# A macaron transformer layer on 8 cores: Q projections fed between the attention windows, double-buffered LayerNorm operands

## What is computed

```python
x = x + 0.5 * ffn(layernorm(x), W_base, b_base, W_router, A, B)
x = x + attn(layernorm(x), Wq, Wk, Wv, Wo)
x = x + 0.5 * ffn(layernorm(x), W_base, b_base, W_router, A, B)

# attn: one K and V head of 128, 32 Q heads of 128, rope on Q and K
for i in range(0, S, 256):                    # windows of 512 tokens
    scores = Qw @ Kw.T * SCALE
    attn = sigmoid(scores); attn = attn / attn.sum(-1)
    wout = attn @ Vw
    # the first half is blended linearly with the last window's second half
return out @ Wo.T
# ffn: x @ W_base.T + b_base + top-2-of-8 gated rank-16 experts
```

## Time and profile before

| | us |
|---|---|
| median of 2 timed runs | 6466.22 (6465.81 to 6466.63) |
| profiled execution, its own time | 6366.92 |
| its span on the slowest core, core 3 | 6365.4 |
| spans of the eight cores | 6328.9 to 6365.4 |

### The profile page before, as it was taken

One profiled execution on the slowest core, in us unless ns is written; L12 is line 12 of the kernel. 1 busy time (PEld: TensorE's weight loads), 2 busy tenths in 40 slices (PEclk: granted clock), 3 DMA queues, 4 the chain that ended last, 5 costly groups with the idle time before them and its releaser, 6 DMA issues.

```text
span 6365.4 us, 39250 instructions; the slowest of 8 cores (6328.9 to 6365.4 us)
## 1 busy us (share of the span) xinstructions
PE 3416.1 (54%) x14036; PEld 1491.5 (23%) x14036; DVE 1207.2 (19%) x1986; ACT 1159.6 (18%) x1401; POOL 523.8 (8%) x900
## 2 busy tenths in 40 slices
PE   2379998344444444444444444444444444425999
PEld 1234443222222111222111222211122211112444
DVE  3511111531121001121100112100121210033111
ACT  3311111322111001212100121100121110022222
POOL 0001111100000110000111000011100011110111
PEclk7689999666665555666665666565666665656999
DMA  4335554321101332100233110133211023332776
GB/s 107 91 96 172 174 168 146 99 75 35 32 27 51 107 107 81 37 27 27 91 107 108 41 37 27 50 104 106 84 30 37 27 83 107 106 110 75 206 200 194
DMA packets 641074, 570.84 MB, mean 90 GB/s; under 512 B 35953, under 2 KB 568690, under 8 KB 640626
## 3 DMA queue, kind: packets, MB, share of 16 engines
q1 hardware_dynamic: 556914, 283.07, 16.5%
q0 software_dynamic: 83968, 285.27, 14.3%
HBM read 459.18 MB, written 109.05 MB: 89 GB/s over the span
## 4 chain that ended last, share of the span: by engine, by line
DMA 35%; PE 32%; DVE 13%; issue 8%; ACT 8%; DVEq 2%; POOL 1%; SPq 0%; POOLq 0%; ACTq 0%
DMA arena<-x2h 13%; PE PS L408 11%; DMA x2h<-arena 10%; PE PS L543 8%; DMA arena<-wqT 5%; DMA arena<-x1h 4%; PE PS L588 4%; PE PS L573 4%; DVE arena L659 3%; DMA out<-arena 2%; ACT arena L577 2%; PE PSM L202 2%; DVEq L47 2%; ACT arena L580 2%; ACT arena L249 2%
## 5 line engine op out<-in xcount | busy, mean ns | idle before, releaser
L652 PE MATMUL PS<-arena 128*128 128x512 bf16 x2048 | 885.9, 611 | 973.1 <-DVE arena L659 966.5
L408 PE MATMUL PS<-arena 128*128 128x512 bf16 x5120 | 1138.1, 381 | 38.6 <-ACT arena L249 25.7
L249 ACT ACTIVATE arena<-arena 128x512 bf16<-128x512 f32 (+1 forms) x784 | 581.2, 765 | 2847.4 <-PE PS L652 1635.0
L543 PE MATMUL PS<-arena 128*128 128x512 bf16 x2048 | 510.5, 416 | 443.6 <-ACT arena L249 407.3
L408 PEld LDWEIGHTS PS<-arena 128*128 128x128 bf16 x5120 | 501.6, 98 | 650.9 <-issue 53.8
L652 PEld LDWEIGHTS PS<-arena 128*128 128x128 bf16 x2048 | 261.3, 136 | 1595.2 <-issue 1587.7
L659 DVE TENSOR_TENSOR arena<-PS,arena 128x512 f32<-128x512 f32 x256 | 177.1, 692 | 1732.6 <-DMA arena<-x2h 1289.5
L202 PE MATMUL PSM<-arena 128*1 128x256 bf16 x1024 | 188.8, 370 | 426.1 <-ACT arena L197 333.8
L43 POOL DMA_DIRECT2D x2h<-arena x256 | 139.6, 545 | 3358.3 <-DVE arena L659 3353.7
L588 PE MATMUL PS<-arena 128*128 128x130 bf16 x2048 | 246.4, 311 | 299.6 <-ACT arena L580 299.6
L543 PEld LDWEIGHTS PS<-arena 128*128 128x128 bf16 x2048 | 212.8, 105 | 735.7 <-issue 538.0
(11 more groups left out here) (85 smaller groups left out, 1879.2 us busy)
## 6 DMA issues: line engine op xcount, KB each, us to landing
arena<-wbaseT SPq DMA_DIRECT2D x256, 512.0 KB, 6.4
arena<-wqT SPq DMA_DIRECT2D x256, 256.0 KB, 3.1
arena<-woT SPq DMA_DIRECT2D x256, 256.0 KB, 3.7
x2h<-arena POOLq DMA_DIRECT2D x256, 256.0 KB, 2.3
arena<-x2h POOLq DMA_DIRECT2D x256, 256.0 KB, 3.2
arena<-xin POOLq DMA_DIRECT2D x24, 1024.0 KB, 11.7
arena<-xin POOLq DMA_DIRECT2D x96, 256.0 KB, 4.6
x1h<-arena POOLq DMA_DIRECT2D x96, 256.0 KB, 2.3
```

The costliest lines, as they stand in the source:

```text
L249: c = pr.emit("scalar", lambda s, si=i % 2, d=dst_bf_ap: s.activation(d, wstage[si], ACT.Copy), wc, 1)
L408: pr.emit("tensor", lambda t, c=c, sl=slot, of=of, t0=t0, n=n: t.matmul(sl, wb[of % 2][:, c, :], xlnb[:, c, t0:t0 + n], start=(c == 0), st ...
L543: qmm[h] = pr.emit("tensor", lambda t, c=c, par=par, hf=hf: t.matmul(PS1[:, hf * 512:(hf + 1) * 512], wqb[par][:, c, :], xlnb[:, c, 256 + ...
L652: mmc = pr.emit("tensor", lambda t, gg=gg, of=of, ts2=ts2, sl=slot: t.matmul(sl[:, 0:512], wqb[of % 2][:, gg, :], wout8[:, gg, ts2 * 512:( ...
```

## The change

There are two parts, in `ln_prep` and in the heads.

In `ln_prep`, `xb` becomes two buffers, and the PSUM tiles alternate: PSM, PS4 for even chunks, PS1, PS2 for odd ones. The casts of a chunk wait for the sums of two chunks before instead of one, and the sums wait for the application of two chunks before.

In the heads, the scores use PS2 alone: two matmuls, a sigmoid, two matmuls in the same banks, a sigmoid. PS1 is left to Q. `qrb` and `sgb` become two buffers each, and the blend gets buffers of its own, which lay in those of rope before. The casts for head h+1 are emitted after rope of head h, ahead of its windows. The 64 matmuls of Q of head h+1 are no longer one block: `feed` places 4 behind the first two scores, 4 behind the second two, and 5 behind the matmuls with V, 13 a window and 64 in five windows. The last head of a group feeds nothing. The first head of groups 1 to 3 gets its casts after the last matmul of Wo, and its Q in one block.

```diff
-        xb = a.bf16(NIF * 256, (NIF, 256))
+        xb = [a.bf16(NIF * 256, (NIF, 256)), a.bf16(NIF * 256, (NIF, 256))]
...
+            ps_st = [PSM[0:1, 0:256], PS1[0:1, 0:256]][par]
+            ps_iv = [PS4[:, 0:128], PS2[:, 0:128]][par]
+            ps_mi = [PSM[:, 0:128], PS1[:, 0:128]][par]
...
-            if i >= 1:
-                wsc.append(("tensor", stats[i - 1]))
-            pr.emit("scalar", lambda s, p=par: s.activation(xb[:, :, 0:128], xf[p], ACT.Copy), wsc, 1)
-            s1 = pr.emit("scalar", lambda s, p=par: s.activation(xb[:, :, 128:256], xf[p], ACT.Square), [], 1)
+            if i >= 2:
+                wsc.append(("tensor", stats[i - 2]))
+            pr.emit("scalar", lambda s, p=par: s.activation(xb[p][:, :, 0:128], xf[p], ACT.Copy), wsc, 1)
+            s1l[i] = s1 = pr.emit("scalar", lambda s, p=par: s.activation(
+                xb[p][:, :, 128:256], xf[p], ACT.Square), [], 1)
             wmm = [("scalar", s1)]
-            if i >= 1:
-                wmm.append(("vector", apply2[i - 1]))
+            if i >= 2:
+                wmm.append(("vector", apply2[i - 2]))
             for c in range(NIF):
-                stats[i] = pr.emit("tensor", lambda t, c=c: t.matmul(
-                    PSM[0:1, 0:256], onesb[:, 0:1], xb[:, c, :],
+                stats[i] = pr.emit("tensor", lambda t, c=c, p=par, ps=ps_st: t.matmul(
+                    ps, onesb[:, 0:1], xb[p][:, c, :],
                     start=(c == 0), stop=(c == NIF - 1)), wmm if c == 0 else [],
...
-        qrb = a.bf16(1024)
+        qrb = [a.bf16(1024), a.bf16(1024)]
...
-        sgb = a.bf16(4 * 512, (4, 512))
+        sgb = [a.bf16(4 * 512, (4, 512)), a.bf16(4 * 512, (4, 512))]
...
-        tb = _resh(qt1, (8, 128))[:, 0:2, :]
-        ub = _resh(qt1, (8, 128))[:, 2:4, :]
-        blb = _resh(qt2[:, 0:128].bitcast(BF16), (2, 128))
+        tb = a.f32(2 * 128, (2, 128))
+        ub = a.f32(2 * 128, (2, 128))
+        blb = a.bf16(2 * 128, (2, 128))
...
+        def stage_wq(h, extra=()):
+            for s8 in range(8):
+                ew = []
+                if h < 2 and s8 == 0:
+                    ew = [("tensor", vmm)]
+                elif s8 == 0:
+                    ew = [("tensor", qmm[h - 2])]
+                ew = ew + (list(extra) if s8 == 0 else [])
+                stage(wqT_r[:, s8 * 4:(s8 + 1) * 4, h * 128:(h + 1) * 128],
+                      wqb[h % 2][:, s8 * 4:(s8 + 1) * 4, :], (), ew)
+            wqc[h] = pr.cnt["scalar"]
+
+        def make_qfeeder(h, extra_first=()):
+            stepctr = {"n": 0}
+
+            def feed(k):
+                while k > 0 and stepctr["n"] < 64:
+                    j = stepctr["n"]
+                    hf, c = j // NIF, j % NIF
+                    w = []
+                    if j == 0:
+                        w = [("scalar", wqc[h]), ("vector", prep_v)] + list(extra_first)
+                        if h >= 1:
+                            w.append(("vector", rope[h - 1]))
+                        if h % 8 == 0 and h > 0:
+                            w.append(("vector", wo_done))
+                        if h == 0:
+                            w.append(("vector", kv_ev))
+                    qmm[h] = pr.emit("tensor", lambda t, c=c, par=h % 2, hf=hf: t.matmul(
+                        PS1[:, hf * 512:(hf + 1) * 512], wqb[par][:, c, :],
+                        xlnb[:, c, 256 + hf * 512:768 + hf * 512],
+                        start=(c == 0), stop=(c == NIF - 1)), w,
+                        1 if (c == NIF - 1 and hf == 1) else 0)
+                    stepctr["n"] += 1
+                    k -= 1
+            return feed
+
+        stage_wq(0)
+        feed = make_qfeeder(0)
+        feed(64)
...
-                for s8 in range(8):
-                    ew = []
-                    if h < 2 and s8 == 0:
-                        ew = [("tensor", vmm)]
-                    elif s8 == 0:
-                        ew = [("tensor", qmm[h - 2])]
-                    stage(wqT_r[:, s8 * 4:(s8 + 1) * 4, h * 128:(h + 1) * 128],
-                          wqb[par][:, s8 * 4:(s8 + 1) * 4, :], (), ew)
-                wq_cast = pr.cnt["scalar"]
-                wmm = [("scalar", wq_cast), ("vector", prep_v), ("scalar", sig_cnt)]
-                if h == 0:
-                    wmm.append(("vector", kv_ev))
-                if hh == 0 and hp > 0:
-                    wmm.append(("vector", wo_done))
-                if h >= 1:
-                    wmm.append(("vector", rope[h - 1]))
-                for hf in range(2):
-                    for c in range(NIF):
-                        qmm[h] = pr.emit("tensor", lambda t, c=c, par=par, hf=hf: t.matmul(
-                            PS1[:, hf * 512:(hf + 1) * 512], wqb[par][:, c, :],
-                            xlnb[:, c, 256 + hf * 512:768 + hf * 512],
-                            start=(c == 0), stop=(c == NIF - 1)),
-                            wmm if (c == 0 and hf == 0) else [],
-                            1 if (c == NIF - 1 and hf == 1) else 0)
-                pr.emit("vector", lambda v: v.tensor_tensor(qt1, PS1[:, 0:1024], cosx[:, 256:1280],
-                                                            ALU.mult), [("tensor", qmm[h])], 1)
+                pr.emit("vector", lambda v, par=par: v.tensor_tensor(
+                    qt1, PS1[:, 0:1024], cosx[:, 256:1280], ALU.mult), [("tensor", qmm[h])], 1)
...
+                rope[h] = pr.emit("vector", lambda v, par=par: v.tensor_tensor(
+                    qrb[par], qt1, qt2, ALU.add), [], 1)
+                if hh < 7:
+                    stage_wq(h + 1)
+                    feed = make_qfeeder(h + 1)
+                else:
+                    feed = lambda k: None
...
-                    slots = [(PS2, 0), (PS2, 512), (PS1, 0), (PS1, 512)]
-                    smm = 0
-                    for kc in range(4):
-                        ps, off = slots[kc]
-                        wsc = []
-                        if kc == 0:
-                            wsc = [("vector", rope[h]), ("scalar", sig_cnt)]
-                        elif kc == 2:
-                            wsc = [("vector", rope[h])]
-                        smm = pr.emit("tensor", lambda t, kc=kc, ps=ps, off=off, q0w=q0w, qn=qn,
-                                      kc0=kc0: t.matmul(
-                            ps[:, off:off + qn], krb[:, (kc0 + kc) * 128:(kc0 + kc + 1) * 128],
-                            qrb[:, q0w:q0w + qn], start=True, stop=True), wsc,
-                            1 if kc == 3 else 0)
-                    pr.emit("scalar", lambda s, qn=qn: s.activation(
-                        sgb[:, 0:2, 0:qn], PS2[:].rearrange("p (c t) -> p c t", c=2)[:, :, 0:qn],
-                        ACT.Sigmoid, scale=SCALE), [("tensor", smm), ("tensor", av_prev)], 1)
-                    sig_cnt = pr.emit("scalar", lambda s, qn=qn: s.activation(
-                        sgb[:, 2:4, 0:qn], PS1[:].rearrange("p (c t) -> p c t", c=2)[:, :, 0:qn],
-                        ACT.Sigmoid, scale=SCALE), [], 1)
+                    sp = wi % 2
+                    w01 = [("vector", rope[h]), ("scalar", sig2_prev)]
+                    for kc in (0, 1):
+                        s01 = pr.emit("tensor", lambda t, kc=kc, q0w=q0w, qn=qn, kc0=kc0, par=par: t.matmul(
+                            PS2[:, kc * 512:kc * 512 + qn], krb[:, (kc0 + kc) * 128:(kc0 + kc + 1) * 128],
+                            qrb[par][:, q0w:q0w + qn], start=True, stop=True),
+                            w01 if kc == 0 else [], 1 if kc == 1 else 0)
+                    feed(4)
+                    wsg1 = [("tensor", s01)]
+                    if (h, wi - 2) in av_hist:
+                        wsg1.append(("tensor", av_hist[(h, wi - 2)]))
+                    elif wi < 2 and h >= 1:
+                        wsg1.append(("tensor", av_hist[(h - 1, 4 - wi)]))
+                    pr.emit("scalar", lambda s, qn=qn, sp=sp: s.activation(
+                        sgb[sp][:, 0:2, 0:qn], PS2[:].rearrange("p (c t) -> p c t", c=2)[:, :, 0:qn],
+                        ACT.Sigmoid, scale=SCALE), wsg1, 1)
+                    sig1 = pr.cnt["scalar"]
+                    for kc in (2, 3):
+                        s23 = pr.emit("tensor", lambda t, kc=kc, q0w=q0w, qn=qn, kc0=kc0, par=par: t.matmul(
+                            PS2[:, (kc - 2) * 512:(kc - 2) * 512 + qn],
+                            krb[:, (kc0 + kc) * 128:(kc0 + kc + 1) * 128],
+                            qrb[par][:, q0w:q0w + qn], start=True, stop=True),
+                            [("scalar", sig1)] if kc == 2 else [], 1 if kc == 3 else 0)
+                    feed(4)
+                    sig_cnt = pr.emit("scalar", lambda s, qn=qn, sp=sp: s.activation(
+                        sgb[sp][:, 2:4, 0:qn], PS2[:].rearrange("p (c t) -> p c t", c=2)[:, :, 0:qn],
+                        ACT.Sigmoid, scale=SCALE), [("tensor", s23)], 1)
+                    sig2_prev = sig_cnt
                     avm = 0
```

(14 more changed lines are left out.)

31 lines of the change are left out of this document (18 added, 13 removed).

## The result

The changed kernel takes 5692.67 us in the median of 11 runs (5641.30 to 5842.98) against 6464.0 for the kernel before. The ratio is 0.8804 with a 95% interval of 0.8741 to 0.8868. One thing is needed to understand the numbers: executions in which the cores of one die run at a lower granted clock than the others are left out of the ratio but not out of the medians; those of the changed kernel that count took 5641 to 5714 us.

The account below looks back on a forecast made before the run. The prediction took the chain of each head (Q, rope, windows, casts) as the changed bound, with Wo held by its slabs. Heads -655, Wo transitions +12 and LayerNorm -15 gave -658 from 6466.2: 5808 us, range 5710 to 6020.

Parts of the forecast that it names:

- The chain of a head: Heads: 71.8 us from rope to rope becomes 49.3 inside a group, 14.5 of casts and 34.8 of windows.
- Cast phase: Heads: ScalarE's eight casts of Q's weights after the last transpose, with TensorE idle; stays at 14.5 us a head.
- The whole term of 655 us: Heads: a group falls from 559.9 to 396.1 us, 163.8 less, four times, 655 in all.
- Which clock: Changed windows: 2.4 GHz assumed, with the first window at 6.1 us, partly at 1.2 GHz.
- the rival that all windows stay at 1.2: Heads: windows take 44.7 us, 9.9 more in 28 heads, total 6085, or 5946 for half; chance 0.16 in full or half.
- the longest hole, 1.9 us: Changed windows at 2.4 GHz: TensorE's longest idle, ahead of the transposes, shorter than 2.45 us survived in the FFN.
- a clock that goes back and forth over short idles: Heads: by the skill's rule, windows would lie between their lengths at the two clocks; not excluded, counted under the second rival.
- Wo to the next group: Between groups: the next head's casts wait for Wo's last matmul; 4 us lost each of three times, 12 in all.
- LayerNorm: LayerNorm stages: the buffers' load cycle keeps its pace, only a 4.9 us lead is won in each of three, 15 us.
- The 99.3 us: Whole kernel: the timed median's excess over the profiled execution, carried over unchanged onto the forecast.
- the unhidden Q: Heads: fed matmuls land where TensorE would have gone on, windows grow to 51 or 52 us, total 6288; chance 0.06.
- the unpipelined short runs: Heads: alternating operands don't stream, each fed matmul costs 0.63 us, windows take 70 us, total 6794; chance 0.03.

Follow-up runs that it names:

- heads alone: The changed kernel with the old `ln_prep`; ratio to the kernel before 0.8974, and 0.8937 when run again on one chip with the changed kernel.
- the wait put back: The changed kernel, but a chunk's sums wait again for the application of the chunk before; ratio to the kernel before 0.8925.
- 0, 0, 13: The changed kernel with all 13 fed matmuls of a window behind those with V, none behind the scores; ratio to the kernel before 0.8984.
- 6, 6, 1: The changed kernel with 6, 6 and 1 fed matmuls in a window instead of 4, 4 and 5; ratio to the kernel before 0.8975.

## Why the prediction was wrong

Point by point, by its own steps:

- **The chain of a head** was right. Cast phase 14.0 us against 14.5; windows of 512 queries 7.7 us, as forecast, and 7.9 for the first of the three; 5.7 for the last against 5.6; first window 5.4 against 6.1 (means of core 3). Heads inside a group are 47.7 to 50.2 us apart there, 48.6 on average, against 49.3. The whole term of 655 us measured 679 on core 3 and 672 on core 0. It was short by 17 to 24, 0.7 us in each of 24 heads the larger part; on core 3 the rest lies in the first group of before, whose eight heads took 569 us where my 71.8 a head stood for 562.
- **Which clock.** I chose 2.4 GHz over the rival that all windows stay at 1.2. It held in 20 of 24 heads, and in 4 but for one dip. My reason for it was not sound, and that it came out is partly luck: I compared the longest hole, 1.9 us, with one of 2.45 survived in the FFN, but 13 matmuls placed otherwise, with no hole over 1.65 us, let the clock fall in every head. What the prediction named from the Trainium skill, TensorE: Matmul & The Clock Gate, section "A second HAM failure mode: psum-queue depth-cycling", a clock that goes back and forth over short idles, is thus seen in the two other placements, once or more in each head at 1.3 to 1.4 us, and rarely in the changed kernel.
- **Wo to the next group.** Forecast 12 us lost. Q's first matmul starts 13.8 us behind the last of Wo instead of 11.9 (rows of core 3 below), in the mean of the three 14.3 instead of 12.2, so some 2 us each time, 6 in all. Wo as a whole, with these transitions, came out 3 to 8 us shorter.
- **LayerNorm** failed in its mechanism. The step that failed is "With two `xf` buffers that pace stays, whatever the sums wait for". I took it from core 3, where a load takes 14 us and the squares of a chunk and the application of the chunk ahead end within 0.1 us of each other on average in the first two stages. On core 0 a load lasts 11.9 us, and the squares end 1.4 to 1.8 us before that application on average: there the sums waited for it, in 27 of 32 chunks, and the cycle of the buffer had slack. After the change the pace is 18.9 to 19.2 us a chunk on average instead of 20.2 to 20.4 (core 0 issues loads at 191.52, 208.35 and 229.19, 16.8 and 20.8 apart by turns). On core 3 the cycle of two chunks went from 41.0 to 37.9 us in the first stage, and 2.0 of that is the load itself, 12.0 instead of 14.0; I had taken its 14 us for a given. The term of 15 us measured 44 to 48.
- **The 99.3 us**, carried over unchanged from the profiled execution to the timed median, was no constant of the kernel, and this is the other step that failed. Of 35 later executions of before, 17 took 6320 to 6380 us, like the profiled one, and seven of the 17 of the changed kernel 5631 to 5648. Its median of 5692.67 lies 51 us above the 5641.6 of its core 3, so of the 99.3 us 48 were too much. That as much as 51 came back is chance: the median execution is the profiled one, and core 5's first FFN made it so long. What lifted the first two timed runs stays open, since their cores' clocks aren't on record. Without the 99 us the range would have been some 5610 to 5920 and held. Its lower end of 5710 was the sum without them, 5709, and so left no room for a term that came out larger.

So the forecast was 115 us too high. Those 48 are one part. The other is in the terms: the sum for the profiled execution was 5709 us, and core 3 ended its span at 5641.6 us, 67 less. On that core heads brought 24 us more than their term, LayerNorm 33 more, and Wo with its transitions 20 more, 77 in all; 19 of them were lost again in the first FFN, at the lower granted clock shown above (772 to 791 us), and 9 came back in the second (541 to 532). Either of the two failed steps, 33 us of LayerNorm or 48 of the 99.3, is more than the 17 us by which the range was missed.

The start of Q behind the last matmuls of Wo, in the timeline of core 3 of the changed kernel, to be held against the earlier trace rows:

```profile
2271.56 3.57 PE L697 MATMUL PS<-arena 128*128 128x512 bf16 x8 [3.95 <-DVE arena L704]
...
2288.97 16.64 PE L559 MATMUL PS<-arena 128*128 128x512 bf16 x64 [13.84 <-ACT arena L256]
```

Of the rivals, the unhidden Q, the clock at 1.2 GHz in all windows and the unpipelined short runs didn't come: four fed matmuls take 1.02 to 1.03 us at 2.4 GHz and 1.91 at 1.2, and V waits for the second sigmoids for 59 us in all instead of 300.

## What to carry to other kernels

Where one engine's block waits for another, its instructions can be spread over the holes of the stage before; what then bounds the stage is the next thing that stood in the same order, here the casts, and moving those brought 207 us more. Read the same wait on several cores before calling it the bound: the slowest core is no typical one, and where it has no margin the others may have slack. And before a timed median is used as a base, hold it against the profiled execution: the 1.6% by which two timed runs lay above it here were no constant to carry over.

## What the runs showed of the hardware

The loads of LayerNorm differ by core, which I hadn't expected. In the first stage of the kernel before, from the end of the application that frees a buffer to the copy of what is loaded into it pass 14.0 us on core 3, 11.9 on core 0 and 11.8 to 13.1 on the other six, for the same 2 MB; in its third stage 11.8 to 12.2 on all eight. In the changed kernel it is 11.8 to 13.3 on average in every stage. It is no matter of core 3 alone: in the first stage of the four traces in which the sums wait for the application ahead (before, heads alone twice, the wait put back), the even cores take 11.6 to 12.0 us and the odd ones 12.4 to 14.0, but for one odd core at 11.9. In the second stage of the eight traces without that wait all cores take 11.6 to 12.4. What lengthens the load on the odd cores stays open; it wasn't tried.

With 4, 4, 5 fed matmuls the granted clock dips in 4 of 24 heads, with 0, 0, 13 and with 6, 6, 1 in all 24, mostly between the V of the third and of the fourth window, 1.3 us each. The mean clock over a long stretch (0.80, 0.81 and 0.77) hardly shows that. The duration of 16 matmuls with V, 1.08 or 1.89 us, shows it only where V falls into the dip: in 12 of the 24 third windows with 0, 0, 13 on core 0, and in none of the changed kernel. Surer is the clock over a few microseconds, as above: 1.00, 0.57, 1.00.

The granted clock of the first FFN was 0.81 on four cores of the changed kernel's profiled execution and 1.00 on core 0 over the same 50 us, with 192 matmuls done instead of 229. It cost cores 2 and 3 some 20 us and cores 4 and 5 some 46.
